# Batch 1's queries and keys made beside batch 0's softmax, in an attention and mixture-of-experts kernel

## The chip, the cores and the metric

The kernel runs on one core of a Trainium2 chip. The metric is device time in microseconds (us) of one execution. Engines are named as in the profile: PE (TensorE; PEld is its weight load), DVE (VectorE), ACT (ScalarE), POOL (GpSimd), SP (SyncE, which here only issues DMAs; its rows are SPq).

## What is computed

```python
def _L0_xattn_ref(teacher_logits, teacher_features, Wq, bq, Wk, bk):
    query = jnp.einsum('bnc,dc->bnd', teacher_features, Wq) + bq
    key = jnp.einsum('bnc,dc->bnd', teacher_features, Wk) + bk
    energy = jnp.einsum('bnd,bmd->bnm', query, key)
    attention = jax.nn.softmax(energy, axis=-1)
    return jnp.einsum('bln,bmn->blm', teacher_logits, attention)

x = x + _L0_xattn_ref(_layernorm(x), ctx_1024, Wq, bq, Wk, bk)
x = x + _L0_ffn_ref(_layernorm(x), ...)   # top 4 of 32 experts, SwiGLU, weighted sum
```

There are 4 batches of 1024 rows with 1024 features; the context has 512 features and queries and keys have 128. The expert part picks 4 of 32 experts for each row from logits that are taken in f32.

## The kernel before

Two functions run one after the other: `attention_and_routing` (the first 716 us) and `experts` (the rest, not touched). In the first, everything goes by tiles of 128 rows, eight tiles a batch, and each engine has a program of its own that is ordered by `schedule`; the engines meet only through semaphores.

`prepare` transposes the weights (into WT and gateT) and the context of batch 0 (`context`, four pairs of tiles, through the PSUM tensor psT into cxT), makes queries and keys (`queries_and_keys`: four quarters of 512 columns, two of queries and two of keys, each of four products, evacuated by DVE into qk at L813) and starts the first `energies`.

A `step(s, b1, b2, more)` then does two things that belong to different batches. The softmax half is for tile s of batch b1: `energies` into psE (L599), maximum (L822) and its negative on DVE, exponent on ACT (L522) into prob, layer norm of x on DVE (L792 to L797, the power of the variance on POOL), the scale of the probabilities (L827, L828), then both results cut into two f16 parts: the high parts on ACT (L529, L531), the low parts on DVE (L834 ah, L837 xnh or xg), and two DMA transposes issued by SP (L408, L413) into AT (printed W) and XT. The product half is for tile s of batch b2: 48 products (L651) into psM, the residual add on DVE (L896, xr, semaphore s_x2), layer norm 2 (LN2, into xs), then one step later its eight transposes on PE (L604, into psT), their evacuation on ACT (L540, x2T), eight logit products (L613) and the top-4 work on DVE.

Three kinds of steps follow each other. In the eight steps of batch 0 there is no product half; below they are called the lone steps. In `both`, from step 1 of the next round on, the LN2 transposes and logit products stand between the 48 products. The last ten steps have only a product half. At step 7 of a round PE makes the next batch's queries and keys and the first energies, in one piece. The context of the next batch is transposed in steps 2 to 5 (`CTX_STEPS`), also in the lone round.

The lines around which the change turns:

```python
quarter = [psM[:, 0:HALF], psM[:, HALF:], psE[:, 0:HALF], psE[:, HALF:]]
held = range(10, 10 + KH)          # LN2 transposes stand before these products of a step's first half
def next_batch():                  # step 7, PE
    alone(pe, s_exp, tile(b1, NT), s_past)
    alone(pe, s_x2, tile(b2, NT), s_past)
    queries_and_keys(following(b1))
```

Of the kernel before, what the change touches and what calls it, by code (L numbers as in the profile page):

```python
# [13 lines left out]
P = 128  # L14
# [119 lines left out]
def attention_and_routing(nc, g):  # L134
# [8 lines left out]
    with ExitStack() as ctx:  # L143
# [79 lines left out]
        quarter = [psM[:, 0:HALF], psM[:, HALF:], psE[:, 0:HALF], psE[:, HALF:]]  # L223
# [11 lines left out]
        s_wTev = sem("w_evacuated")  # L235
        s_x2out = [sem(f"x2_out{t}") for t in range(2)]
# [48 lines left out]
        CTX_STEPS = range(2, 2 + NT // 2)  # L285

# [20 lines left out]
        def lagged(bk, s, lag):  # L307

            if bk is None:
                return None  # L310
            if s >= lag:
                return (bk, s - lag) if s - lag < NT else None
            return None if first(bk) else ((bk[0], bk[1] - 1), NT + s - lag)

# [31 lines left out]
        def _(sp):  # L346
# [10 lines left out]
            sp.dma_start(wqk_in[:, 0, :], g["Wq"]).then_inc(s_small, 16)  # L357
            sp.dma_start(wqk_in[:, 1, :], g["Wk"]).then_inc(s_small, 16)
# [4 lines left out]
            load_ctx(0)  # L363
# [134 lines left out]
        def _(act):  # L498
            for n in range(2 * KC + KH):
                act.wait_ge(s_wT, n + 1)  # L500
                if n < 2 * KC:
                    act.activation(WT[:, n // KC, n % KC, :], psT[:, n % 2 * HALF:n % 2 * HALF + D], ACT.Copy).then_inc(s_wTev, 1)
                else:
                    act.activation(gateT[:, n - 2 * KC, :], psT[:, n % 2 * HALF:n % 2 * HALF + E], ACT.Copy).then_inc(s_wTev, 1)

            def context(bk, pair):
                act.wait_ge(s_cT, per(NT // 2, bk, pair + 1))
                act.activation(cxT[:, :, pair * 2 * P:(pair + 1) * 2 * P].rearrange("p c (t q) -> p t c q", t=2),
                               psT[:, :].rearrange("p (t c q) -> p t c q", t=2, c=KC), ACT.Copy).then_inc(s_cTev, 1)

            def prepare():
                for pair in range(NT // 2):
                    context((0, 0), pair)
                act.wait_ge(s_padout, 16 * 5)

            def step(s, b1, b2, more):
# [31 lines left out]
                if b1 is not None:  # L548
                    guarded(act, own, exponent)
                    if b2 is None and s - 1 in CTX_STEPS:  # L550
                        context(following(b1), s - 1 - CTX_STEPS[0])
# [30 lines left out]
        def _(pe):  # L582
            pe.wait_ge(s_const, 8)
            pe.wait_ge(s_small, 16 * 6)
            for n in range(2 * KC + KH):
                if n >= 2:
                    pe.wait_ge(s_wTev, n - 1)
                dst = psT[:, n % 2 * HALF:]
                if n < 2 * KC:
                    pe.transpose(dst[:, 0:D], wqk_in[:, n // KC, n % KC * P:(n % KC + 1) * P], ident[:]).then_inc(s_wT, 1)  # L590
                else:
                    k = n - 2 * KC
                    pe.transpose(dst[:, 0:E], gate_in[:, k * P:(k + 1) * P], ident[0:E, 0:E]).then_inc(s_wT, 1)
            pe.wait_ge(s_wTev, 2 * KC + KH)
# [22 lines left out]
            def context(bk, pair):  # L617

                if pair == 0:
                    alone(pe, s_ctx, per(16, bk, 16), s_past)  # L620
                for t in range(2):
                    for c in range(KC):
                        op = pe.transpose(psT[:, t * HALF + c * P:t * HALF + (c + 1) * P],
                                          cx[:, 2 * pair + t, c * P:(c + 1) * P], ident[:])
                op.then_inc(s_cT, 1)

            def queries_and_keys(bk):

                pe.wait_ge(s_cTev, per(NT // 2, bk, NT // 2))
                for n in range(4):  # L630
                    for c in range(KC):
                        op = pe.matmul(quarter[n], WT[:, n // 2, c, :], cxT[:, c, n % 2 * HALF:(n % 2 + 1) * HALF],
                                       start=c == 0, stop=c == KC - 1)
                    op.then_inc(s_qk, 1)
                pe.wait_ge(s_qkev, per(4, bk, 4))
                energies(0)

            def prepare():
                for pair in range(NT // 2):
                    if pair:  # L640
                        pe.wait_ge(s_cTev, pair)
                    context((0, 0), pair)
                queries_and_keys((0, 0))

# [66 lines left out]
            def step(s, b1, b2, more):  # L711
# [38 lines left out]
                if b1 is not None:  # L750
                    if s in CTX_STEPS:
                        if s - 1 in CTX_STEPS:
                            pe.wait_ge(s_cTev, per(NT // 2, following(b1), s - CTX_STEPS[0]))
                        guarded(pe, more, lambda: context(following(b1), s - CTX_STEPS[0]))
                if b2 is not None and s < NT:
                    product(product_of(s, b1), b2, s, 1, range(KH // 2, KH)).then_inc(s_xm, 1)
                if b1 is not None:
                    if b2 is not None:
                        guarded(pe, own, next_energies)
                    if s == NT - 1:  # L760
                        def next_batch():

                            alone(pe, s_exp, tile(b1, NT), s_past)
                            if b2 is not None:
                                alone(pe, s_x2, tile(b2, NT), s_past)
                            queries_and_keys(following(b1))
                        guarded(pe, more, next_batch)
# [14 lines left out]
        def _(dve):  # L782
# [24 lines left out]
            dve.wait_ge(s_small, 16 * 6)  # L807
            dve.wait_ge(s_wTev, 2 * KC + KH)

            def queries_and_keys(bk):  # L810
                for n in range(4):
                    dve.wait_ge(s_qk, per(4, bk, n + 1))
                    dve.tensor_scalar(qk[:, n // 2, n % 2 * HALF:(n % 2 + 1) * HALF], quarter[n],  # L813
                                      bqk[:, n // 2:n // 2 + 1], None, ALU.add).then_inc(s_qkev, 1)

            def step(s, b1, b2, more):
                own = more if s < 2 else None

                def maximum_and_norm():
# [3 lines left out]
                    dve.tensor_scalar(nmx[:, 0:1], mx[:, 0:1], -1.0, None, ALU.mult).then_inc(s_nmx, 1)  # L823
                    dve.wait_ge(s_x1[s % 2], per(8 * NT, b1, 16 * (s // 2 + 1)))
# [6 lines left out]
                def lo_parts():  # L831
# [42 lines left out]
                if b1 is not None:  # L874
# [435 lines left out]
```

## Time and profile before

| | us |
|---|---|
| median of 3 runs | 3167.7 (3167.55 to 3170.44) |
| time of the profiled execution | 3168.07 |
| its span in the profile | 3166.0 |
| PE busy | 3023.1 (95%) |
| DVE busy | 1710.9 (54%) |
| ACT busy | 1187.7 (38%) |
| POOL busy | 562.4 (18%) |

The busy shares are means over stages with different limits, so the table alone says little about the first 716 us: there, each stretch has to be read by itself. In a row of a timeline the first number is the start, the second how long the row lasts, then engine, line, operation, and in brackets how long the engine had been idle and whose result ended that.

### The profile page before, as it was taken

Reading aid. Unit: us, or ns where it says so; the run is one execution under the profiler, and the core shown is the slowest. Engines: PE = TensorE matmul, PEld = TensorE weight load, DVE = VectorE, ACT = ScalarE, POOL = GpSimd, SP = SyncE. Lnnn points to the kernel's source line nnn. Section 1 sums busy time; section 2 is a strip of 40 time slices with the busy share of each in tenths; the row PEclk is TensorE's granted clock in tenths of the full one; section 3 lists DMA queues with packets and bytes.
Section 4 is the critical chain, followed back from the end, with each engine's and each line's share of the span. In section 5 each row is a group of like instructions: output and inputs, shape, how many; then the busy total and the mean of one; then the engine's idle time right before and its main releaser. Section 6 shows DMA issues by size and latency. Waiting matters only on the chain.

```text
span 3166.0 us, 44613 instructions
## 1 busy us (share of the span) xinstructions
PE 3023.1 (95%) x14944; PEld 1547.1 (49%) x14945; DVE 1710.9 (54%) x2851; ACT 1187.7 (38%) x1235; POOL 562.4 (18%) x502
## 2 busy tenths in 40 slices
PE   6798988979999999999999999999999999999997
PEld 2354544544454454455445445445455544544543
DVE  3687878664454544555544545555454544554532
ACT  2342423223343434344443434444343433442422
POOL 1022323331111111111111111111111111111111
PEclk8899999989999999999999999999999999999999
DMA  6766656555554555656555656665556555565432
GB/s 191 176 176 184 176 145 182 159 167 161 158 153 113 163 151 154 196 159 179 171 141 153 195 146 190 183 186 152 155 161 191 153 155 157 153 180 132 116 64 60
DMA packets 343541, 501.36 MB, mean 158 GB/s; under 512 B 190881, under 2 KB 190881, under 8 KB 343234
## 3 DMA queue, kind: packets, MB, share of 16 engines
q10 hardware_dynamic: 94576, 225.46, 21.5%
q0 software_dynamic: 45856, 152.33, 21.3%
q1 hardware_dynamic: 203058, 122.94, 14.7%
q8 instruction: 25, 0.41, 0.1%
q14 instruction: 26, 0.21, 0.0%
HBM read 354.64 MB, written 112.46 MB: 148 GB/s over the span
## 4 chain that ended last, share of the span: by engine, by line
PE 75%; DMA 1%; issue 0%; ACT 0%; DVE 0%; SPq 0%; POOL 0%; ACTq 0%; POOLq 0%
PE psG L1226 23%; PE psU L1226 23%; PE psY L1248 23%; PE psX L1232 4%; PE psA L1239 2%; DMA acc<-y,idxs 0%; DMA idxs<-slots 0%; DMA stage<-in_L_ffn_w_gate 0%; ACT xT L1092 0%; DVE y L1171 0%; ACT y L1103 0%; POOL acc L1083 0%; SPq L1019 0%; ACTq L1016 0%; SPq L1020 0%
## 5 line engine op out<-in xcount | busy, mean ns | idle before, releaser
L1226 PE MATMUL psG<-W,xT 128*128 128x512 f16 x3456 | 770.8, 379 | 2.9 <-ACT xT L1092 2.8
L1248 PE MATMUL psY<-W,aT 128*128 128x512 f16 x3456 | 769.4, 379 | 1.5 <-ACT aT L1096 1.4
L1226 PE MATMUL psU<-W,xT 128*128 128x512 f16 x3456 | 769.4, 379 | 0.0
L1226 PEld LDWEIGHTS psG<-W,xT 128*128 128x128 f16 x3456 | 338.1, 98 | 412.3 <-issue 3.9
L1248 PEld LDWEIGHTS psY<-W,aT 128*128 128x128 f16 x3456 | 338.0, 98 | 377.3 <-ACT aT L1096 1.9
L1226 PEld LDWEIGHTS psU<-W,xT 128*128 128x128 f16 x3456 | 338.1, 98 | 375.7
L127 DVE SCALAR_TENSOR_TENSOR W<-stage,W 128x2048 f16<-128x2048 f32 x192 | 438.6, 2284 | 6.9 <-ACT W L122 6.7
L1171 DVE SCALAR_TENSOR_TENSOR y<-bias,idxs,y 128x1024 f32<-128x1024 f32 x143 | 183.7, 1285 | 462.3 <-ACT y L1103 462.3
L1059 POOL DMA_INDIRECT acc<-y,idxs x143 | 224.9, 1573 | 1006.4 <-DVE y L1171 966.9
L122 ACT ACTIVATE W<-stage 128x2048 f16<-128x2048 f32 x192 | 365.9, 1905 | 51.0 <-issue 38.2
L651 PE MATMUL psM<-W,XT 128*128 128x512 f16 x1392 | 355.9, 379 | 8.6 <-DVE xr L896 8.6
L1103 ACT ACTIVATE y<-psY,idxs 128x1024 f32<-128x1024 f32 x143 | 159.3, 1114 | 521.6 <-DMA idxs<-slots 518.2
L1054 POOL DMA_INDIRECT xg<-xn_tab,idxg x145 | 154.0, 1062 | 1051.7 <-PE psX L1232 649.0
L1092 ACT ACTIVATE xT<-psX 128x1024 f32<-128x1024 f32 x145 | 148.6, 1025 | 435.0 <-PE psX L1232 434.8
L1179 DVE SCALAR_TENSOR_TENSOR gt<-psG,bias 128x512 f32<-128x512 f32 x144 | 99.6, 692 | 364.6 <-PE psG L1226 340.4
L1190 DVE SCALAR_TENSOR_TENSOR up<-psU,bias 128x512 f32<-128x512 f32 x144 | 99.6, 692 | 301.0 <-PE psU L1226 301.0
L1139 ACT ACTIVATE sg<-gt 128x512 f32<-128x512 f32 x144 | 90.8, 631 | 444.1 <-DVE gt L1182 443.9
L651 PEld LDWEIGHTS psM<-W,XT 128*128 128x128 f16 x1392 | 149.4, 110 | 128.8 <-DVE xr L896 11.2
L485 POOL DMA_INDIRECT slots<-pack,dest x128 | 139.5, 1090 | 207.8 <-DVE tok L871 169.9
L1232 PE MATMUL psX<-ident,xg 128*128 128x128 f32 x1160 | 151.2, 274 | 15.6 <-PEq L143 15.6
L1232 PEld LDWEIGHTS psX<-ident,xg 128*128 128x128 f32 x1160 | 136.5, 142 | 44.2 <-DMA xg<-xn_tab,idxg 16.5
L522 ACT ACTIVATE stage<-psE,nmx 128x1024 f32<-128x1024 f32 x32 | 35.7, 1115 | 254.3 <-DVE nmx L823 254.3
(140 smaller groups left out, 2180.8 us busy)
## 6 DMA issues: line engine op xcount, KB each, us to landing
stage<-in_L_ffn_w_down ACTq DMA_DIRECT2D x62, 1024.0 KB, 6.3
stage<-in_L_ffn_w_up ACTq DMA_DIRECT2D x61, 1024.0 KB, 7.4
stage<-in_L_ffn_w_gate ACTq DMA_DIRECT2D x60, 1024.0 KB, 9.5
stage<-in_x SPq DMA_DIRECT2D x32, 512.0 KB, 5.3
xr<-in_x SPq DMA_DIRECT2D x32, 512.0 KB, 4.6
acc<-xr SPq DMA_DIRECT2D x32, 512.0 KB, 3.9
xn_tab<-x2h SPq DMA_DIRECT2D x32, 512.0 KB, 3.0
bias<-in_L_ffn_b_down ACTq DMA_DIRECT2D x32, 512.0 KB, 7.1
```

The source lines that it names most:

```text
L122: act.activation(W[:, par, HI, c * CHUNK:(c + 1) * CHUNK], stage[:, c % RING, :], ACT.Copy, scale=S_W).then_inc(s_whi, 1)
L127: dve.scalar_tensor_tensor(out=W[:, par, LO, c * CHUNK:(c + 1) * CHUNK], in0=stage[:, c % RING, :], scalar=S_W, in1=W[:, par, HI, c * CHUN ...
L485: pool.indirect_dma_start(out=slots[:, :], out_offset=bass.IndirectOffsetOnAxis(dest[:, n % 2, k:k + 1], 0), in_=pack[:, n % 2, k, :], in_ ...
L651: op = pe.matmul(out[:, h * HALF:(h + 1) * HALF], XT[:, a, k, t * P:(t + 1) * P], AT[:, par(bk), c, k, h * HALF:(h + 1) * HALF].rearrange( ...
L1054: pool.indirect_dma_start(out=xg[:], out_offset=None, in_=xn_tab[:, :], in_offset=bass.IndirectOffsetOnAxis(idxg[:, 0:1].bitcast(U32), 0)) ...
L1059: pool.indirect_dma_start(out=acc[:, :], out_offset=bass.IndirectOffsetOnAxis(idxs[:, 0:1].bitcast(U32), 0), in_=y[:], in_offset=None, com ...
L1092: act.activation(xT[:].rearrange("p k q a -> p (k q a)").bitcast(F32), psX[:], ACT.Copy).then_inc(s_xTev, 1)
L1103: act.activation(y[:], psY[:], ACT.Copy, scale=idxs[:, 2:3].bitcast(F32)).then_inc(s_y0, 1)
L1171: dve.scalar_tensor_tensor(out=y[:], in0=bias[:, par, 2 * I:], scalar=idxs[:, 1:2].bitcast(F32), in1=y[:], op0=ALU.mult, op1=ALU.add).then ...
L1226: op = pe.matmul(ps[:], xT[:, k, :, a], weights(par, c, offset + k * I, I), start=k == 0 and n == 0, stop=k == KH - 1 and n == 2)
L1232: op = pe.transpose(psX[:, n * P:(n + 1) * P], xg_w[:, n * P:(n + 1) * P], ident[:])
L1248: op = pe.matmul(psY[:, h * HALF:(h + 1) * HALF], aT[:, k, :, a], weights(par, c, 2 * KH * I + k * H + h * HALF, HALF), start=k == 0 and n ...
```

## The change

It has four parts, all in `attention_and_routing`.

1. **Start.** Wq and Wk get a semaphore of their own (s_wqk), and the context of batch 0 is loaded third on SP and not seventh. The eight weight transposes go into all of psT and leave in one evacuation. The four context pairs go into psM, psE, psT and psM, so only the fourth waits for an evacuation. The gate's transposes move behind the queries and keys.
2. **Lone round.** The context of batch 1 is transposed in steps 0 to 3, and one quarter of its queries and keys is made in each of steps 4 to 7, into the halves of psM, psQ and psR. DVE does the low parts of tile s-1 after the maximum of tile s (in step 7 also its own low parts), and the exponent waits for the low part of the probabilities, since it overwrites prob. At the end of step 7 only the four evacuations and the first energies are left.
3. **LN2 transposes** in `both` stand before products 16 to 23 and no longer 10 to 17, and the logit products before products 4 to 11 of the second half and no longer 2 to 9.
4. **Batches 2 and 3.** The queries' two quarters go into psE, and wait only for the last exponent; the keys' quarters go into psM and wait for the residual add (s_x2).

```diff
-        quarter = [psM[:, 0:HALF], psM[:, HALF:], psE[:, 0:HALF], psE[:, HALF:]]
+        psE_halves, psM_halves = [[ps[:, 0:HALF], ps[:, HALF:]] for ps in (psE, psM)]
+        early = psM_halves + [psQ[:, :], psR[:, :]]
+        first_pairs = [psM, psE, psT, psM]
...
+        CTX_ALONE = range(NT // 2)
+        QK_ALONE = range(NT // 2, NT)
+        QK_ORDER = (0, 2, 1, 3)
...
+        def quarter(bk, n):
+
+            if batch(bk) == 0:
+                return (psM_halves + psE_halves)[n]
+            return early[n] if batch(bk) == 1 else (psE_halves + psM_halves)[n]
...
-            sp.dma_start(wqk_in[:, 0, :], g["Wq"]).then_inc(s_small, 16)
-            sp.dma_start(wqk_in[:, 1, :], g["Wk"]).then_inc(s_small, 16)
+            sp.dma_start(wqk_in[:, 0, :], g["Wq"]).then_inc(s_wqk, 16)
+            sp.dma_start(wqk_in[:, 1, :], g["Wk"]).then_inc(s_wqk, 16)
+            load_ctx(0)
...
-            load_ctx(0)
...
                 def exponent():
                     act.wait_ge(s_nmx, tile(b1, s + 1))
+                    act.wait_ge(s_alo, tile(b1, s))
...
             def queries_and_keys(bk):
 
                 pe.wait_ge(s_cTev, per(NT // 2, bk, NT // 2))
                 for n in range(4):
...
+                    if n == 0 and not first(bk):
+                        pe.wait_ge(s_exp, NT * batch(bk))
+                    if n == 2 and not first(bk):
+                        pe.wait_ge(s_x2, NT * (batch(bk) - 1))
+                    one_quarter(bk, n)
...
-                held = range(10, 10 + KH)
+                held = range(16, 16 + KH)
...
-                    if m == 2:
+                    if m == 4:
...
-                    if 2 <= m < 2 + KH:
-                        logits_block(m - 2)
+                    if 4 <= m < 4 + KH:
+                        logits_block(m - 4)
...
+                if b1 is not None and b2 is None:
+                    if s == 0:
+                        pe.wait_ge(s_wTev, 2)
+                    if s in CTX_ALONE:
+                        if s > 0:
+                            pe.wait_ge(s_cTev, per(NT // 2, following(b1), s))
+                        context(following(b1), s)
+                    if s in QK_ALONE:
+                        n = QK_ORDER[s - QK_ALONE[0]]
+                        pe.wait_ge(s_cTev, per(NT // 2, following(b1), NT // 4 * (n % 2 + 1)))
+                        one_quarter(following(b1), n)
...
                     if s == NT - 1:
-                        def next_batch():
-
-                            alone(pe, s_exp, tile(b1, NT), s_past)
-                            if b2 is not None:
-                                alone(pe, s_x2, tile(b2, NT), s_past)
-                            queries_and_keys(following(b1))
-                        guarded(pe, more, next_batch)
+                        pe.wait_ge(s_exp, tile(b1, NT))
+                        first_energies(following(b1))
...
                     dve.tensor_scalar(nmx[:, 0:1], mx[:, 0:1], -1.0, None, ALU.mult).then_inc(s_nmx, 1)
+                    if b2 is None and s > 0:
+                        lo_parts(s - 1)
...
-                if b1 is not None:
+                if b1 is not None and (b2 is not None or s == NT - 1):
                     guarded(dve, own, lo_parts)
```

**Where instructions move.** First PE's program at the very start; stage holds the weights as loaded, W the context. Before:

```order
L590 MATMUL psT<-ident,stage 128x128 [waits small_in,consts]
L590 MATMUL psT<-ident,stage 128x128
L590 MATMUL psT<-ident,stage 128x128 [waits w_evacuated] x6
L593 MATMUL psT<-ident,stage 128x32 [waits w_evacuated] x8
L623 MATMUL psT<-ident,W 128x128 [waits ctx_in,w_evacuated,dve_consts]
L623 MATMUL psT<-ident,W 128x128 x7
L623 MATMUL psT<-ident,W 128x128 [waits ctxT_evacuated]
```

The same stretch of the changed kernel:

```order
L601 MATMUL psT<-ident,stage 128x128 [waits wqk_in,consts]
L601 MATMUL psT<-ident,stage 128x128 x7
L633 MATMUL psM<-ident,W 128x128 [waits ctx_in,w_evacuated,dve_consts]
L633 MATMUL psM<-ident,W 128x128 x7
L633 MATMUL psE<-ident,W 128x128 x8
L633 MATMUL psT<-ident,W 128x128 x8
L633 MATMUL psM<-ident,W 128x128 [waits ctxT_evacuated]
```

Twenty-four context transposes now stand in a row without a wait, and the gate's eight have gone behind the queries and keys.

Second, DVE's program in one lone step, from one maximum to the next. Before:

```order
L822 TENSOR_REDUCE mx<-psE 128x1 [waits energy_done]
L823 TENSOR_SCALAR nmx<-mx 128x1 [waits softmax_chain]
L792 BN_STATS st<-stage 128x6 [waits x1_in1]
L792 BN_STATS st<-stage 128x6
L794 BN_AGGR mv<-st 128x2 [waits ln1_chain]
L795 TENSOR_SCALAR ve<-mv 128x1 [waits ln1_chain]
L797 TENSOR_SCALAR stage<-stage,mv,rstd 128x1024 [waits rstd1_ready]
L827 RECIPROCAL sc<-psm 128x1 [waits exp_done]
L828 TENSOR_SCALAR sc<-sc 128x1 [waits softmax_chain]
L834 SCALAR_TENSOR_TENSOR ah<-stage,sc,ah 128x1024 [waits prob_scale_ready,prob_hi]
L837 SCALAR_TENSOR_TENSOR xg<-stage,xg 128x1024 [waits ln1_hi]
L822 TENSOR_REDUCE mx<-psE 128x1 [waits energy_done]
```

In the changed kernel:

```order
L845 TENSOR_REDUCE mx<-psE 128x1 [waits energy_done]
L846 TENSOR_SCALAR nmx<-mx 128x1 [waits softmax_chain]
L859 SCALAR_TENSOR_TENSOR ah<-stage,sc,ah 128x1024 [waits prob_scale_ready,prob_hi]
L862 SCALAR_TENSOR_TENSOR xnh<-stage,xnh 128x1024 [waits ln1_hi]
L815 BN_STATS st<-stage 128x6 [waits x1_in1]
L815 BN_STATS st<-stage 128x6
L817 BN_AGGR mv<-st 128x2 [waits ln1_chain]
L818 TENSOR_SCALAR ve<-mv 128x1 [waits ln1_chain]
L820 TENSOR_SCALAR stage<-stage,mv,rstd 128x1024 [waits rstd1_ready]
L852 RECIPROCAL sc<-psm 128x1 [waits exp_done]
L853 TENSOR_SCALAR sc<-sc 128x1 [waits softmax_chain]
L845 TENSOR_REDUCE mx<-psE 128x1 [waits energy_done]
```

The two low parts, which belong to the tile before, have come between the negative maximum and the statistics.

Third, PE's program from the last lone energies to the first products. Before, it is eight products into psM and eight into psE in one piece. In the changed kernel:

```order
L608 MATMUL psE<-stage 128x512 [waits exp_done]
L608 MATMUL psE<-stage 128x512
L639 MATMUL psM<-W,WT 128x512 [waits ctxT_evacuated]
L639 MATMUL psM<-W,WT 128x512 x3
L639 MATMUL psR<-W,WT 128x512 [waits ctxT_evacuated]
L639 MATMUL psR<-W,WT 128x512 x3
L608 MATMUL psE<-stage 128x512 [waits qk_evacuated,exp_done]
L608 MATMUL psE<-stage 128x512
L675 MATMUL psM<-W,XT 128x512 [waits ln1T_in0,probT_in1,probT_in0]
```

The last two quarters (steps 6 and 7) now stand ahead of the wait for the evacuations, and nothing but the energies is behind it. PE's products count twice in the trace: one f32 product of 512 columns shows as two rows' worth (x2).

## Rows read from the trace of the kernel before

**Rows 1.** The page, part 4: the chain that ended last, by line.

```profile
PE psG L1226 23%; PE psU L1226 23%; PE psY L1248 23%; PE psX L1232 4%; PE psA L1239 2%; DMA acc<-y,idxs 0%; DMA idxs<-slots 0%; DMA stage<-in_L_ffn_w_gate 0%; ACT xT L1092 0%; DVE y L1171 0%; ACT y L1103 0%; POOL acc L1083 0%; SPq L1019 0%; ACTq L1016 0%; SPq L1020 0%
```

**Rows 2.** Windows: length, busy us of each engine, PE's granted clock, DMA share, GB/s.

```profile
0.00:46.87 46.87, 31.64 (x84) 16.86 (x85) 7.35 (x12) 8.94 (x22) 5.75 (x20) 1.00 0.59 216
46.87:106.37 59.50, 30.55 (x60) 13.77 (x60) 44.12 (x77) 26.76 (x32) 3.86 (x7) 0.67 0.77 168
106.37:128.89 22.52, 18.88 (x37) 7.96 (x38) 9.39 (x16) 3.30 (x4) 0.55 (x1) 0.81 0.91 210
128.89:569.18 440.29, 394.63 (x2012) 225.44 (x2010) 348.57 (x1061) 144.82 (x196) 123.44 (x134) 1.00 0.64 170
```

**Rows 3.** DMA issues (KB, median us to landing) and PE's timeline, 0 to 45 us.

```profile
W<-in_ctx SPq DMA_DIRECT2D x2, 2048.0 KB, 9.9
stage<-in_L_xattn_Wk SPq DMA_DIRECT2D x1, 256.0 KB, 3.1
14.70 1.94 PE L623 MATMUL psT<-ident,W 128*128 128x128 f32 x8 [1.81 <-DMA W<-in_ctx]
...
27.00 10.13 PE L632 MATMUL psM<-W,WT 128*128 128x512 f32 x16 [1.11 <-ACT W L508]
...
44.85 1.98 PE L599 MATMUL psE<-stage 128*128 128x512 f32 x4 [0.84 <-DVE stage L813]
```

**Rows 4.** Timeline of one lone step (s = 1), from maximum to maximum.

```profile
55.33 1.22 DVE L822 TENSOR_REDUCE mx<-psE 128x1 f32<-128x1024 f32 x1
...
56.65 1.27 DVE L792 BATCH_NORM_STATS2 st<-stage 128x6 f32<-128x512 f32 x2
56.77 1.11 ACT L522 ACTIVATE stage<-psE,nmx 128x1024 f32<-128x1024 f32 x1 [2.86 <-DVE nmx L823]
...
58.03 3.78 PE L599 MATMUL psE<-stage 128*128 128x512 f32 x4 [5.07 <-ACT stage L522]
...
60.07 0.15 DVE L828 TENSOR_SCALAR sc<-sc 128x1 f32<-128x1 f32 x1
...
61.44 1.28 DVE L834 SCALAR_TENSOR_TENSOR ah<-stage,sc,ah 128x1024 f16<-128x1024 f32 x1 [1.22 <-ACT ah L529]
...
63.77 1.22 DVE L822 TENSOR_REDUCE mx<-psE 128x1 f32<-128x1024 f32 x1
```

**Rows 5.** Window over the same step, columns as in rows 2.

```profile
55.33:63.77 8.44, 3.78 (x4) 1.17 (x4) 6.30 (x12) 3.30 (x4) 0.55 (x1) 0.60 0.87 186
```

**Rows 6.** Timeline of step 7 of the lone round: queries and keys, and SP.

```profile
109.16 10.00 PE L632 MATMUL psM<-W,WT 128*128 128x512 f32 x16 [5.57 <-ACT stage L522]
...
113.87 7.51 SPq L408 DMA_TRANSPOSE W<-ah  x1
```

**Rows 7.** Timeline of PE where batches 2 and 3 begin.

```profile
261.57 8.80 PE L632 MATMUL psM<-W,WT 128*128 128x512 f32 x16 [3.21 <-DVE xr L896]
...
278.08 1.98 PE L599 MATMUL psE<-stage 128*128 128x512 f32 x4 [0.84 <-DVE stage L813]
...
416.93 7.10 PE L632 MATMUL psM<-W,WT 128*128 128x512 f32 x16 [3.18 <-DVE xr L896]
...
431.74 1.98 PE L599 MATMUL psE<-stage 128*128 128x512 f32 x4 [0.84 <-DVE stage L813]
```

**Rows 8.** PE's waits between 128 and 620 us, and one `both` step.

```profile
PE psT L604 <- DVE xs L797: 25.2, 21, 1.3
...
173.95 2.33 PE L651 MATMUL psM<-W,XT 128*128 128x512 f16 x10 [0.37 <-DVE xr L896]
...
177.62 0.30 PE L604 MATMUL psT<-ident,xs 128*128 128x128 f32 x1 [1.34 <-DVE xs L797]
...
181.14 1.00 ACT L540 ACTIVATE x2T<-psT 128x1024 f32<-128x1024 f32 x1
...
182.19 0.41 PE L613 MATMUL psR<-gateT,x2T 128*128 128x32 f32 x2
...
190.18 1.22 DVE L896 SCALAR_TENSOR_TENSOR xr<-psM,xr 128x1024 f32<-128x1024 f32 x1
```

More of the change, by code:

```diff
@@ L498, in _ @@
         def _(act):
[L499 to L504, printed above, removed]
+            act.wait_ge(s_wT, 1)
+            act.activation(WT[:, :, :, :].rearrange("p w c d -> p (w c d)"), psT[:], ACT.Copy).then_inc(s_wTev, 1)
             def context(bk, pair):
                 act.wait_ge(s_cT, per(NT // 2, bk, pair + 1))
+                ps = first_pairs[pair] if first(bk) else psT
                 act.activation(cxT[:, :, pair * 2 * P:(pair + 1) * 2 * P].rearrange("p c (t q) -> p t c q", t=2),
-                               psT[:, :].rearrange("p (t c q) -> p t c q", t=2, c=KC), ACT.Copy).then_inc(s_cTev, 1)
+                               ps[:, :].rearrange("p (t c q) -> p t c q", t=2, c=KC), ACT.Copy).then_inc(s_cTev, 1)
             def prepare():
@@ L549, in step @@
                     guarded(act, own, exponent)
-                    if b2 is None and s - 1 in CTX_STEPS:
-                        context(following(b1), s - 1 - CTX_STEPS[0])
+                    if b2 is None and s - 1 in CTX_ALONE:
+                        context(following(b1), s - 1)
                 if late:
@@ L583, in _ @@
             pe.wait_ge(s_const, 8)
[L584 to L594, printed above, removed]
+            pe.wait_ge(s_wqk, 16 * 2)
+            for n in range(2 * KC):
+                op = pe.transpose(psT[:, n * D:(n + 1) * D], wqk_in[:, n // KC, n % KC * P:(n % KC + 1) * P], ident[:])
+            op.then_inc(s_wT, 1)
+            pe.wait_ge(s_wTev, 1)
             pe.wait_ge(s_ready, 1)
@@ L620, in context, with one_quarter @@
                     alone(pe, s_ctx, per(16, bk, 16), s_past)
+                ps = first_pairs[pair] if first(bk) else psT
                 for t in range(2):
                     for c in range(KC):
-                        op = pe.transpose(psT[:, t * HALF + c * P:t * HALF + (c + 1) * P],
+                        op = pe.transpose(ps[:, t * HALF + c * P:t * HALF + (c + 1) * P],
                                           cx[:, 2 * pair + t, c * P:(c + 1) * P], ident[:])
                 op.then_inc(s_cT, 1)
+            def one_quarter(bk, n):
+                for c in range(KC):
+                    op = pe.matmul(quarter(bk, n), WT[:, n // 2, c, :], cxT[:, c, n % 2 * HALF:(n % 2 + 1) * HALF],
+                                   start=c == 0, stop=c == KC - 1)
+                op.then_inc(s_qk, 1)
             def queries_and_keys(bk):
@@ L630, in queries_and_keys, with first_energies @@
                 for n in range(4):
[L631 to L634, printed above, removed]
+                    if n == 0 and not first(bk):
[3 more added lines that the diff above has]
+                    one_quarter(bk, n)
+            def first_energies(bk):
                 pe.wait_ge(s_qkev, per(4, bk, 4))
@@ L639, in prepare @@
                 for pair in range(NT // 2):
-                    if pair:
-                        pe.wait_ge(s_cTev, pair)
+                    if pair == 3:
+                        pe.wait_ge(s_cTev, 1)
                     context((0, 0), pair)
                 queries_and_keys((0, 0))
+                pe.wait_ge(s_small, 16 * 4)
+                for k in range(KH):
+                    op = pe.transpose(psT[:, k * E:(k + 1) * E], gate_in[:, k * P:(k + 1) * P], ident[0:E, 0:E])
+                op.then_inc(s_wT, 1)
+                first_energies((0, 0))
             def product(out, bk, t, h, blocks, beside=None):
@@ L806, in _ @@
             dve.memset(psm[:], 0.0).then_inc(s_seen, 1)
-            dve.wait_ge(s_small, 16 * 6)
-            dve.wait_ge(s_wTev, 2 * KC + KH)
+            dve.wait_ge(s_small, 16 * 4)
+            dve.wait_ge(s_wTev, 1)
             def queries_and_keys(bk):
-                for n in range(4):
-                    dve.wait_ge(s_qk, per(4, bk, n + 1))
-                    dve.tensor_scalar(qk[:, n // 2, n % 2 * HALF:(n % 2 + 1) * HALF], quarter[n],
+                for done, n in enumerate(quarter_order(bk)):
+                    dve.wait_ge(s_qk, per(4, bk, done + 1))
+                    dve.tensor_scalar(qk[:, n // 2, n % 2 * HALF:(n % 2 + 1) * HALF], quarter(bk, n),
                                       bqk[:, n // 2:n // 2 + 1], None, ALU.add).then_inc(s_qkev, 1)
```

15 lines of the change are left out of this document (7 added, 8 removed).

## The prediction

> **What bounds the kernel now.** I read the chain that ended last first. It is PE nearly throughout, in lines of the experts [rows 1], which the change does not touch: their 2450 us move as a block. So only the first 716 us can change, and what is won there is won in full, since the experts begin when routing is done. The windows split that part [rows 2]. In the start (0 to 46.87) and in the lone round (46.87 to 106.37) PE is busy for 31.6 and 30.6 us only and no engine is full: these are chains of waits. Step 7 of the lone round takes 22.52 us, 18.88 of them PE's. The product rounds (128.89 to 569.18) look like PE's at 394.6 of 440.3 us, but the step itself says otherwise: DVE's residual add at 190.18 had no idle time before it, so DVE came straight from other work, while PE waited 0.37 us for it at 173.95 and 1.34 us for LN2 at 177.62 [rows 8]. DVE is the bound there, and PE's 25.2 us of waits for LN2 are mostly slack.
>
> **Start.** Before, PE waits for the context until 14.70, transposes four pairs with an evacuation behind each, starts queries and keys at 27.00 and the first energies at 44.85 [rows 3]. The context is now issued third, about 1.9 us earlier; a 2 MB load lands a median 9.9 us after issue [rows 3], and I take a start of the transposes at 12.2. The weights land 3.1 us after issue [rows 3], long before. Three of four pairs no longer wait: 4 x 1.94 = 7.8 us [rows 3], then one evacuation, for which I take the 1.1 us of idle ahead of 27.00 [rows 3]: queries and keys start near 20.8. Sixteen pieces took 10.13 us there at first, where PE had been interrupted before, and 7.10 us at 416.93 where it was warm [rows 3, 7]. The granted clock reads 1.00 over the whole start [rows 2], but 10.13 against 7.10 us for the same pieces means that part of them ran at 1.2 GHz. With 32 transposes in one run ahead of them I expect the 2.4 GHz pace from the first one: 431.74 - 416.93 = 14.8 us to the first energies [rows 7]. That gives 35.6, or **9.3 us** less. Bounds: context at 13.5 and the slow pace kept (17.85 us) give 4.5 us; context at 11.1 and fast transposes give 11.3 us. The gate's eight transposes hide behind the last evacuation (0.84 us idle [rows 3]).
>
> **Lone round.** DVE's chain from maximum (55.33) to the end of the scale (60.22) is 4.89 us; from the low part (61.44) to the next maximum (63.77) 2.33 us [rows 4]. What goes is the wait for ACT's high part between them, 1.22 us, because it now falls under the next maximum. DVE's cycle becomes 4.89 + 2.33 = 7.2 us against 8.44 [rows 5]. But the exponent now stands behind the low part: it starts at 1.33 (statistics at 56.65 less 55.33) + 1.28 = 2.65 us after the maximum, not at 1.44; the energies follow 1.26 us behind (56.77 to 58.03) and take 3.78 us [rows 4]: the next maximum can start at 7.7. So the loop through PE, at a granted clock of 0.60 [rows 5], is the longer one; at the 1.98 us of warm energies [rows 7] it would be 5.9 and DVE's 7.2 decides. DMA is third: a share of 0.87 of 8.44 us [rows 5] is 7.3 us of work in a step, mostly transposes. Steps 1 to 3, with 2 us of context transposes each, I put at 7.6. In step 4 a quarter follows the energies: eight pieces at 10.13/16 to 0.85 us are 5 to 6.8 us, so PE is busy on end, rises to 2.4 GHz (sixteen pieces in 10.00 us at 109.16, in 7.10 warm [rows 6, 7], say it does within them), and steps 5 and 6 go at DVE's or DMA's 7.3. Step 0 has no low parts before its statistics: exponent at once, 6.1 us. Sum for the seven steps: 6.1 + 4 x 7.6 + 2 x 7.3 = 51.1 against 59.50 [rows 2]: **8.4 us**. Bounds: all at 7.75 gives 6.9, all at DVE's 7.2 about 10.
>
> The Trainium skill, page "DMA: Bandwidth & Descriptors", section "Latency and other measured facts", gives 261 GB/s for a DMA transpose. By that figure the 1 MB of a step would be an estimated 4 us and DMA would be no bound; the step's rows show 186 GB/s at a share of 0.87, so the measurement decides, and DMA stays in the sum at 7.3.
>
> **Step 7 of the lone round.** After its maximum DVE does the low parts of tile 6, its own statistics and scale (7.1), waits for the high part, its own low parts (8.5 to 10.9), then four evacuations of ready quarters, 0.7 us each: energies at 13.7. PE has been idle for some 8 us then, so they cost 3.78, not 1.98: next maximum at 17.4 against 22.52 [rows 2], 5.1 us less. The first products then start at the low clock too, 1.2 us lost. The ctx load and the last probability transposes (issued 7.51 us long at 113.87 [rows 6]) land near 20 us, before the second half of the products asks for them near 23. Net **3.9 us**, bounds 2 and 5.
>
> **Batches 2 and 3.** PE is idle 3.21 and 3.18 us for the residual add, then needs 16.51 and 14.81 us to the energies [rows 7]; the first time the clock has dropped (8.80 us for sixteen pieces against 7.10). Now the queries start when the products end, at 258.4 and 413.8, and PE stays warm. The products themselves end 0.4 us earlier, as two more stand ahead of the logits. Energies at 272.9 and 428.2: 5.2 and 3.5 us, less 0.1 each for a later x2T: **8.5 us**, bounds 7 and 9.5.
>
> **LN2 transposes six products later.** From 173.95 sixteen products (0.21 us each, 10 in 2.33) reach 177.4, so the wait of 1.34 us nearly goes [rows 8]. But x2T is evacuated at 181.14 because ACT has the exponent and x2h before it, and logits start at 182.19 either way; the transposes, done near 180.2, leave 0.9 us. And DVE's loop does not pass through them. I give it 0.2 us in the one step where DVE still waited for PE, and nothing in the other 22.
>
> Sum: 9.3 + 8.4 + 3.9 + 8.5 + 0.2 = 30.3 us. The sum is made against the profiled execution's 3168.07, which is 0.4 above the median of the runs: **3137.8 us**. The terms' bounds add up to 20.4 and 36.0 us, 3132 to 3148.
>
> **Rivals.** (a) *DMA becomes the bound.* With the share at 1 the transposes of the lone round queue up, the low parts' buffers come free late, and step 7's land after the products want them, behind the 2 MB context. The share was 0.91 in that step [rows 2], which speaks for it; that each transpose has more than a step until it is needed speaks against it. Lone steps at 8.2 leave 2 us of 8.4 and the transition nothing: 30.3 - 10.3 = 20 us, 3148. (b) *PE stays at 1.2 GHz.* Quarters at 6.8 us and energies at 3.78 make steps 4 to 6 PE's, 10.6 us each, 3 x 3.1 = 9.3 us lost, 3 more in the start: 18 us, 3150. Against it: PE rose within sixteen pieces both times [rows 3, 6]. The Trainium skill, page "TensorE: Matmul & The Clock Gate", section "HAM oscillation — how this bites in real kernels", warns that idle gaps between bursts throw PE back to 1.2 GHz again and again, which speaks against handing out the quarters one by one; that is this rival, and the trace agrees that lone energies are slow (clock 0.60). (c) *Slower.* If the postponed LN2 transposes end more than 0.9 us later than I put them, x2T, logits and then every one of the 23 `both` steps grow. It decides from 0.9 + 30.3/23 = 2.2 us: at 3 us, 23 x 2.1 - 30.3 = 18 us slower, 3186. Nothing in the rows makes them that late. (d) *No change*: the experts would have to wait for something other than routing; the chain shows no such wait [rows 1]. 3168.
>
> **How the numbers follow.** Forecast 0.80, (a) 0.08, (b) 0.05, (c) 0.03, (d) 0.02, and 0.02 for a gain over 36 us. Of this kernel a measurement tells 0.2% (6 us) from no change. Forecast, (a) and (b) are all faster: 0.94; no change 0.03 and slower 0.03. The range goes from 3131 to 3149, to take in (a) and the low bounds.
>
> **What would show it.** First energies near 35.6; maxima of the lone round 7.2 to 7.8 apart, with DVE's idle before the low part gone and a new one before the maximum where PE is slow; the maximum of step 7 and of the next step 17.4 apart; no idle of PE after the last product of a batch; residual adds in `both` as far apart as before and PE's wait for LN2 replaced by one before the logits. I am wrong if PE keeps the low clock through queries and keys at the start, or if steps 5 and 6 stand above 8.

## The result, and the profile after

The changed kernel takes 3136.78 us, median of 4 runs (3135.79 to 3139.09), against 3168.56 for the one before (median of 4 runs). The ratio is 0.9902, 95% interval 0.9889 to 0.9914: it is faster, by some 31.8 us, with 3137.8 predicted. The profiled execution took 3135.79 us, its span is 3133.8.

The same windows as in [rows 2], cut at the corresponding maxima and residual adds (columns as there):

```profile
0.00:35.83 35.83, 23.57 (x84) 13.65 (x85) 7.36 (x11) 6.58 (x8) 5.76 (x20) 1.00 0.75 282
35.83:86.07 50.24, 34.43 (x80) 16.32 (x81) 41.82 (x75) 24.66 (x30) 3.86 (x7) 0.80 0.85 181
86.07:103.65 17.58, 9.47 (x19) 3.69 (x18) 11.43 (x19) 5.40 (x6) 0.55 (x1) 0.73 1.07 260
103.65:535.11 431.46, 393.04 (x2012) 224.54 (x2010) 348.24 (x1061) 144.70 (x196) 123.45 (x134) 1.00 0.68 176
```

The four stretches have lost 11.0, 9.3, 4.9 and 8.8 us, 34.1 together. The experts' first transposes start at 682.41, from where the window to the end of the span is 2451.39 us long; before it was 2449.78 us (from 716.22). So 1.6 us came back behind the change, and 0.3 us more between the last of these windows and the experts (147.30 us against 147.04). Most of the 1.6 us is in one place: the first 24 products of the experts took 7.98 us and not 6.69. That is a varying clock and not the change: in another profile of the changed kernel (e12_changed_again) the same products took 6.83 us.

**Start.** PE's timeline; the rows answer to [rows 3]. A "piece" is one row of PE's in the trace (the x16 at the end of a line are sixteen of them); "warm" below means the pace at 2.4 GHz and "cold" that at 1.2 GHz.

```profile
12.72 1.94 PE L633 MATMUL psM<-ident,W 128*128 128x128 f32 x8 [6.40 <-DMA W<-in_ctx]
14.46 1.56 PE L633 MATMUL psE<-ident,W 128*128 128x128 f32 x8
15.86 1.04 PE L633 MATMUL psT<-ident,W 128*128 128x128 f32 x8
16.73 1.04 PE L633 MATMUL psM<-ident,W 128*128 128x128 f32 x8
18.97 7.13 PE L639 MATMUL psM<-W,WT 128*128 128x512 f32 x16 [1.20 <-ACT W L520]
...
33.81 1.98 PE L608 MATMUL psE<-stage 128*128 128x512 f32 x4 [0.24 <-DVE stage L836]
```

Eight transposes take 1.94 us at first and 1.04 us from the third pair on: that is the step from 1.2 to 2.4 GHz, in the transposes and no longer in the products, whose first sixteen pieces take 7.13 us.

**Lone round.** One step's timeline, against [rows 4]:

```profile
56.51 1.23 DVE L845 TENSOR_REDUCE mx<-psE 128x1 f32<-128x1024 f32 x1 [0.38 <-PE psE L608]
57.85 1.28 DVE L859 SCALAR_TENSOR_TENSOR ah<-stage,sc,ah 128x1024 f16<-128x1024 f32 x1
59.23 1.11 ACT L537 ACTIVATE stage<-psE,nmx 128x1024 f32<-128x1024 f32 x1 [0.89 <-DVE ah L859]
60.19 1.28 DVE L815 BATCH_NORM_STATS2 st<-stage 128x6 f32<-128x512 f32 x2
60.49 3.37 PE L608 MATMUL psE<-stage 128*128 128x512 f32 x4 [3.08 <-ACT stage L537]
63.89 1.23 DVE L845 TENSOR_REDUCE mx<-psE 128x1 f32<-128x1024 f32 x1
```

The low part has no idle time ahead of it any more. In its place DVE waits 0.38 us for the energies, since the exponent now starts 2.72 us after the maximum (59.23 less 56.51), behind the low part. Here is how the maxima stand apart in the two lone rounds, and behind them the two steps in which batch 1 begins (from the starts of L822 and L845):

| | s=0 | 1 | 2 | 3 | 4 | 5 | 6 | 7 | next |
|---|---|---|---|---|---|---|---|---|---|
| before | 8.46 | 8.44 | 8.52 | 8.52 | 8.53 | 8.51 | 8.52 | 22.52 | 15.04 |
| changed | 5.80 | 7.24 | 7.64 | 7.38 | 7.80 | 7.18 | 7.20 | 17.58 | 15.42 |

**Step 7.** PE, SP and DVE:

```profile
88.14 3.60 PE L639 MATMUL psR<-W,WT 128*128 128x512 f32 x8
...
93.57 0.70 SPq L370 DMA_DIRECT2D W<-in_ctx  x1
94.39 0.57 SPq L367 DMA_DIRECT2D stage<-in_x  x1
95.97 9.08 SPq L423 DMA_TRANSPOSE W<-ah  x1
...
99.85 3.75 PE L608 MATMUL psE<-stage 128*128 128x512 f32 x4 [8.11 <-DVE stage L836]
...
103.65 1.22 DVE L845 TENSOR_REDUCE mx<-psE 128x1 f32<-128x1024 f32 x1 [3.94 <-PE psE L608]
```

The queries and keys are done 8.11 us before the energies need them, and the energies then run at 1.2 GHz.

**Batches 2 and 3.** PE's timeline, against [rows 7]:

```profile
232.53 7.03 PE L639 MATMUL psE<-W,WT 128*128 128x512 f32 x16
239.40 7.03 PE L639 MATMUL psM<-W,WT 128*128 128x512 f32 x16
247.27 1.98 PE L608 MATMUL psE<-stage 128*128 128x512 f32 x4 [0.84 <-DVE stage L836]
...
382.59 7.03 PE L639 MATMUL psE<-W,WT 128*128 128x512 f32 x16
```

No idle time, and full pace from the first piece. The transition, from the maximum of step 7 to the first maximum of the next batch, now takes 27.1 us both times; it took 32.68 and 30.96.

**`both` steps.** PE's waits between 104 and 595 us, and one step, against [rows 8]:

```profile
PE psR L622 <- ACT x2T L555: 18.9, 21, 1.0
PE psM L675 <- DVE xr L921: 11.0, 20, 1.0
...
139.28 0.41 PE L622 MATMUL psR<-gateT,x2T 128*128 128x32 f32 x2 [0.70 <-ACT x2T L555]
```

The 25.2 us of waits for LN2 have become 18.9 us of waits for x2T and more for the residual add; the maxima of these steps still stand 17.5 us apart.

### The profile page after: what moved, and what is told of

The parts are those of the page before. It is cut to its first block, busy times and chain, and to the rows that moved or that the text cites. A ratio compares the mean times of both kernels' runs of the same rounds, so it can differ in the third digit from the quotient of the medians.

```text
span 3133.8 us, 44628 instructions
## 1 busy us (share of the span) xinstructions
PE 3009.1 (96%) x14944; PEld 1541.6 (49%) x14945; DVE 1710.8 (55%) x2851; ACT 1184.7 (38%) x1221; POOL 562.5 (18%) x502
## 4 chain that ended last, share of the span: by engine, by line
PE 77%; DMA 1%; issue 0%; ACT 0%; POOL 0%; ACTq 0%; DVE 0%; SPq 0%; POOLq 0%
PE psG L1251 24%; PE psU L1251 24%; PE psY L1273 23%; PE psX L1257 4%; PE psA L1264 2%; DMA stage<-in_L_ffn_w_gate 0%; DMA idxs<-slots 0%; DMA acc<-y,idxs 0%; ACT xT L1117 0%; POOL acc L1108 0%; DVE y L1196 0%; ACTq L1041 0%; ACT y L1128 0%; SPq L1044 0%; SPq L1045 0%
## 5 line engine op out<-in xcount | busy, mean ns | idle before, releaser
L1225 DVE SCALAR_TENSOR_TENSOR ahl<-av,ahl 128x512 f16<-128x512 f32 x144 | 105.4, 732 | 43.1 <-ACT ahl L1170 43.1
```

## The experiments

Each is an edit of the changed kernel, unless it says otherwise. Medians of one and the same kernel differ by 1 to 1.5 us between sets of runs (the changed kernel gave 3136.78 and 3137.96, the one before 3168.56 to 3170.0), so where a few us or less are at stake I go by the distances between maxima in the profile, which repeat within 0.05 us wherever PE's clock is the same.

**e1_ln2_back.** The LN2 shift undone.

```diff
-                held = range(16, 16 + KH)
+                held = range(10, 10 + KH)
-                    if m == 4:
+                    if m == 2:
-                    if 4 <= m < 4 + KH:
-                        logits_block(m - 4)
+                    if 2 <= m < 2 + KH:
+                        logits_block(m - 2)
```

> The changed kernel with its third part undone: LN2 transposes again before products 10 to 17, logits before products 2 to 9. My theory: DVE bounds these steps, PE's 25 us of waits for LN2 were slack; the median moves from 3136.8 to between 3136.5 and 3138, PE waits for xs again (about 1.3 us, 20 times) and residual adds stay as far apart. Rival: the moved transposes are part of the gain; then the time rises by up to 25 us, to 3150 or more.

3138.55 us, half a us above the range I had given and, at that spread, not told apart from the changed kernel. Its waits (104 to 600 us) are those of the kernel before:

```profile
PE psT L613 <- DVE xs L820: 25.2, 21, 1.3
```

and the steps are as far apart as with the shift, 17.5 us. What the shift moves is small and of both signs: the transitions take 27.54 and 27.53 instead of 27.10 us (the two products ahead of the logits), the first `both` step takes 15.76 instead of 15.41, but the step behind each transition takes 17.53 instead of 17.83. The rival of 25 us falls.

**e2_low_back.** The low parts back in their own step.

```diff
-                    if b2 is None and s > 0:
-                        lo_parts(s - 1)
-                if b1 is not None and (b2 is not None or s == NT - 1):
+                if b1 is not None:
```

> The changed kernel with the low parts of a lone step back in their own step, behind ACT's high part. Theory: lone steps return from 7.2 to 7.8 to 8.45 us (+9.1 over seven steps), while step 7 loses the 2.3 us of tile 6's low parts: +6.8, near 3143.6. Rival: DMA, at a share near 1 in these steps, is what spaces them; then the steps stay at 7.2 to 7.8 and the time falls by 2 us or stays.

3144.26 us. The lone steps take 8.44 to 8.53 us again and step 7 takes 15.17 us. So the whole gain per lone step is DVE's order; at that spacing the quarters and transposes beside it cost nothing.

**e3_qk_end.** All four quarters in step 7.

```diff
-                    if s in QK_ALONE:
-                        n = QK_ORDER[s - QK_ALONE[0]]
-                        pe.wait_ge(s_cTev, per(NT // 2, following(b1), NT // 4 * (n % 2 + 1)))
-                        one_quarter(following(b1), n)
+                    if s == NT - 1:
+                        pe.wait_ge(s_cTev, per(NT // 2, following(b1), NT // 2))
+                        for n in QK_ORDER:
+                            one_quarter(following(b1), n)
```

> The changed kernel, but all four quarters of batch 1's queries and keys in one piece in step 7 (their banks are free, so they still start before the last exponent). Theory: queries and keys need 17 us from the end of the last energies, first 1.2 then 2.4 GHz; maximum of step 7 to the next maximum 19.9 instead of 17.6, energies of steps 4 to 6 slow again (+1.1 in all), the products after them warm (-0.4): +3.0, near 3139.8. Rival: handing out the quarters one by one is the source of the whole gain there; then the distance returns to 22.5 and the time rises by 5 to 6 us. Other rival: handing them out costs clock; then it gets faster.

3139.27 us, within the spread of the changed kernel. In the profile step 7 takes 17.82 us, hardly more than 17.58, because the first quarter starts at 89.34 already, before that step's maximum (89.58), and warms up in 4.83 us:

```profile
89.34 4.83 PE L639 MATMUL psM<-W,WT 128*128 128x512 f32 x8
...
94.00 3.60 PE L639 MATMUL psQ<-W,WT 128*128 128x512 f32 x8
97.44 3.60 PE L639 MATMUL psM<-W,WT 128*128 128x512 f32 x8
...
100.87 3.60 PE L639 MATMUL psR<-W,WT 128*128 128x512 f32 x8
...
105.40 1.96 PE L608 MATMUL psE<-stage 128*128 128x512 f32 x4 [0.94 <-DVE stage L836]
```

The energies are then warm (1.96 us) and the step behind takes 15.02; steps 4 to 6 take 7.84, 7.72 and 7.81. Together with the step behind, that is 1.0 us slower, not 3.0. So step 7's gain comes from banks that are free: the products no longer wait for the last exponent. Handing them out over four steps adds about 1 us.

**e4_bank_back.** Batches 2 and 3 wait for the residual add first.

```diff
-            return early[n] if batch(bk) == 1 else (psE_halves + psM_halves)[n]
+            return early[n] if batch(bk) == 1 else (psM_halves + psE_halves)[n]
...
-                        pe.wait_ge(s_exp, NT * batch(bk))
+                        pe.wait_ge(s_x2, NT * (batch(bk) - 1))
...
-                        pe.wait_ge(s_x2, NT * (batch(bk) - 1))
+                        pe.wait_ge(s_exp, NT * batch(bk))
```

> The changed kernel with batches 2 and 3 again as before: queries into psM behind the residual add, keys into psE. Theory: PE is idle for 3.6 us again, the first time cold for 1.7 us, and each of the two transitions gets back what it won, 5.6 and 3.9 us: +9.4, near 3146.2. Rival: DVE's LN2 and evacuations set the end of these transitions, and the bank is worth less than 4 us.

3149.4 us, 12.6 more where I expected 9.4. The transitions take 32.68 and 34.00 us: 5.6 and 6.9 us more. The mechanism is as expected, with a larger second price, because this time the clock was low there too (before, these sixteen pieces took 7.10 us [rows 7]):

```profile
237.65 8.80 PE L639 MATMUL psM<-W,WT 128*128 128x512 f32 x16 [3.64 <-DVE xr L921]
...
393.31 10.12 PE L639 MATMUL psM<-W,WT 128*128 128x512 f32 x16 [3.64 <-DVE xr L921]
```

**e5_load_back.** The first context load seventh again (`load_ctx(0)` behind the load of gb).

> The changed kernel with the context of batch 0 loaded seventh again, behind the small loads. Theory: context transposes start at 14.6 and not 12.7, everything behind them shifts by 1.9 us: near 3138.7. Rival: the landing is set by the DMA engines and not by the issue, no change.

3138.23 us. The transposes start at 14.08. In the ten profiles whose start is that of the changed kernel they start anywhere from 12.61 to 14.26, 13.5 on average. The early load is issued 1.88 us sooner (at 1.85 and not 3.73), but it took 10.5 to 12.2 us to land in those ten and 10.1 us here. Inconclusive: the landing alone varies by 1.7 us, nearly as much as the earlier issue could win. Neither my theory nor the rival is shown.

**e6_pairs_back.** Four pairs through one bank pair.

```diff
-        first_pairs = [psM, psE, psT, psM]
+        first_pairs = [psT, psT, psT, psT]
...
-                    if pair == 3:
-                        pe.wait_ge(s_cTev, 1)
+                    if pair:
+                        pe.wait_ge(s_cTev, pair)
```

> The changed kernel with all four first context pairs through psT again, each behind the evacuation of the one before. Theory: transposes take 12.3 us and not 6.2 to the start of queries and keys (+6.1), and PE, interrupted, starts these at 1.2 GHz: their first sixteen pieces take 10.1 and not 7.0 us (+3.1): +9.2, near 3146.0. Rival: the clock rises by itself after the start whatever the transposes do; then only +6.1, near 3142.9.

3146.64 us. PE's timeline:

```profile
12.87 1.94 PE L633 MATMUL psT<-ident,W 128*128 128x128 f32 x8 [6.48 <-DMA W<-in_ctx]
15.93 1.97 PE L633 MATMUL psT<-ident,W 128*128 128x128 f32 x8 [1.11 <-ACT W L520]
...
25.17 9.74 PE L639 MATMUL psM<-W,WT 128*128 128x512 f32 x16 [1.11 <-ACT W L520]
```

The transposes start like the changed kernel's, but queries and keys start at 25.17 and not 18.97, and run their first sixteen pieces in 9.74 us and not 7.13. Interrupted transposes keep PE at 1.2 GHz. The products pay 2.6 us for it, and so do the transposes themselves: from their start to that of queries and keys PE is busy for 7.84 us here and for 5.05 us in the changed kernel, so of the 6.1 us between the two 2.8 are clock and only 3.3 are waits. The total is as expected, its parts are not: 5.4 us of clock and 3.3 of waits.

**e7_warm.** Eight unused products in the gap of step 7. They are added work and change no result.

```diff
                         pe.wait_ge(s_exp, tile(b1, NT))
+                        for _ in range(8):
+                            pe.matmul(psE[:, 0:HALF], WT[:, 0, 0, :], cxT[:, 0, 0:HALF], start=True, stop=True)
                         first_energies(following(b1))
```

> The changed kernel with eight unused f32 products of 512 columns into psE between the last quarter and the first energies of batch 1 (they write a bank that the energies write again). Theory: PE's 8.1 us of idle time cost it the clock; with them the energies take 1.98 and not 3.75 us and the next products run at 2.4 GHz: -2.2, near 3134.6. Rival: the products end after the evacuations and delay the energies, or the clock changes nothing; then 3136.8 or more.

3135.52 us.

```profile
99.50 1.98 PE L608 MATMUL psE<-stage 128*128 128x512 f32 x4 [1.16 <-DVE stage L838]
101.33 5.34 PE L675 MATMUL psM<-W,XT 128*128 128x512 f16 x24
...
107.42 5.34 PE L675 MATMUL psM<-W,XT 128*128 128x512 f16 x24 [0.75 <-DMA W<-ah]
```

The energies are warm and step 7 takes 15.72 us, 1.9 less. But the next step takes 15.93 and not 15.42: the second half of the products waits 0.75 us for the last probability transposes. A wait that was hidden has come out, and 1.3 us are left where I expected 2.2.

**e8_dma_more.** One more 512 KB load in each lone step, into x2h and xs2, which are unused there. (Lines that are not shown make ACT and DVE wait for these loads before the buffers are used again; the last load landed at 113.0, before the products that this run is about were done, so these waits are not what it measures.)

```diff
+                    if b2 is None:
+                        dst = (x2h[:, 0, :, :], x2h[:, 1, :, :])[s % 3] if s % 3 < 2 else xs2[:, :]
...
+                        sp.dma_start(dst, x_rows[0, s]).then_inc(s_extra[s % 3], 16)
```

> The changed kernel with one more load of 512 KB in each lone step, into buffers that are unused there. It adds some 1.4 us of work of all DMA engines to the 7.3 us of a step. Theory: transposes are not needed until two steps later, so the first lone steps keep 7.2 to 7.8 us, the backlog grows by 1.4 us a step, and only step 7 and the products behind it feel it: +3 to +8. Rival: DMA already bounds the lone steps; then each grows by 1.4 us, +11. Other rival: DMA is far from the bound, less than +1.

3146.43 us, 9.7 more, which is above my +3 to +8 and near the rival's +11. The steps tell the two apart: the lone ones behind step 0 take 7.18 to 7.84 us and step 7 17.58, as without the loads, but the step behind it 23.09 instead of 15.42:

```profile
101.67 10.99 SPq L424 DMA_TRANSPOSE W<-ah  x1
104.47 6.64 PE L686 MATMUL psM<-W,XT 128*128 128x512 f16 x24
...
114.91 8.20 PE L686 MATMUL psM<-W,XT 128*128 128x512 f16 x24 [3.80 <-DMA W<-ah]
```

The backlog is paid in one place, where the products first ask for tile 7's probabilities. It shows in SP's issues too: the last transpose of probabilities begins to be issued 14.5 us after the maximum of step 7 and not 9.9. The 7.7 us are 3.8 of wait and 3.9 of clock, for the first 24 products (6.64 us) and above all the second (8.20), against 5.34 warm. The clock is what I had left out.

**e9_ctx_late.** e7_warm, and the 2 MB context load behind step 7's transposes.

```diff
-                    if s == NT - 2:
+                    if s == NT - 1:
                         guarded(sp, None if first(b1) else b1[0] < B - 3, next_ctx)
```

> e7_warm with the 2 MB load of the next-but-one context issued behind the transposes of step 7 and not ahead of them. In e7_warm PE waited 0.75 us for the last probability transposes, which stood 11.7 us in the queue. Theory: that wait goes and they land within 6 us of issue; from the first maximum of batch 1 to the next 15.0 instead of 15.9: -0.9 against e7_warm, near 3134.5. Rival: the transposes are slow by themselves or the load then delays the next ones; no change.

3134.54 us, ratio 0.9891 (0.9875 to 0.9908).

```profile
96.87 2.98 SPq L423 DMA_TRANSPOSE W<-ah  x1
...
101.54 1.29 SPq L370 DMA_DIRECT2D W<-in_ctx  x1
102.49 10.52 PE L675 MATMUL psM<-W,XT 128*128 128x512 f16 x48
```

The transpose of tile 7's probabilities landed 4.9 us after its issue, in the changed kernel 11.2. The forty-eight products run without a break and the step takes 15.03 us, 0.9 less than in e7_warm, as expected.

**e10_lone_warm.** e9_ctx_late with one unused product in each of steps 0 to 3.

```diff
                         context(following(b1), s)
+                        pe.matmul(psR[:, :], WT[:, 0, 0, :], WT[:, 1, :, :].rearrange("p c d -> p (c d)"), start=True, stop=True)
```

> e9_ctx_late with one unused f32 product of 512 columns behind the context transposes of each of steps 0 to 3, into psR. Theory: PE is busy in some 80% of a step instead of 62% and keeps 2.4 GHz more often; energies take 1.98 and not 3.2 to 3.8 us, the maxima stand 7.2 apart, up to 1.5 us less than e9_ctx_late. Rival: the gap ahead of the energies remains, the clock falls as before, and the added product only stands in their way: 0 to +2.

3135.3 us. Steps 1 to 4 take 7.58, 7.18, 7.83 and 7.18 us, 29.8 together, in e9_ctx_late 7.41, 7.82, 7.18 and 7.20, 29.6. Nothing is won: PE still idles 2.3 to 3.5 us ahead of the energies, which took 3.56, 1.98 and 3.78 us in turn.

**e11_start_warm.** e9_ctx_late with three unused products of the same form while PE waits for the first context.

> e9_ctx_late with three unused f32 products into psR while PE waits for the first context (6.4 us idle). Theory: the context transposes start at 2.4 GHz and ACT's evacuations (four times 1.1 us) bound them: the first maximum comes at 35 to 36 in every profile and not anywhere from 35.8 to 38.8 as in the kernels so far: -1 to -2 against e9_ctx_late. Rival: the spread comes from when the context lands; no change.

3134.65 us. All four pairs take 1.04 to 1.07 us and the first maximum comes at 34.7, against 38.13 in e9_ctx_late. But step 0 takes 6.58 instead of 4.84 us and steps 3 and 4 are slow, so that at the maximum of step 7 only 1.3 us are left (85.7 against 87.0), and the median shows none of it. The spread of the start has two sources, then: when the context lands, and when PE rises to 2.4 GHz in the transposes (from their start to that of queries and keys the ten profiles take 6.25 to 7.70 us, this one 4.93).

**e12_changed_again.** The changed kernel, beside the last three.

> The changed kernel itself, beside e9 to e11 on the same chip. Its median should be 3136 to 3138. Its first maximum was at 35.83 in its profile, the earliest of seven kernels that start alike; I expect it nearer 37.3 this time, with the lone steps and transitions as before within 0.6 us.

3137.96 us. The first maximum comes at 38.39, then the steps take 4.84, 7.62, 7.81, 7.18, 7.84, 7.17, 7.20, 17.40 and 15.03 us. Step 0 is 0.96 us shorter than in the first profile, more than the 0.6 I allowed; the others lie within it. Beside it e9_ctx_late is 3.4 us faster (3133.61 to 3135.64 against 3137.79 to 3139.28). It is the best version found, though e10_lone_warm and e11_start_warm are not told apart from it.

## Why the prediction was right

| term | predicted | profile of the change |
|---|---|---|
| start | 9.3 | 11.0 (46.87 - 35.83) |
| lone round | 8.4 | 9.3 (59.50 - 50.24) |
| step 7, and the clock behind it | 3.9 | 4.6 (22.52 - 17.58 less 15.42 - 15.04) |
| batches 2 and 3 | 8.5 | 8.8 (5.58 + 3.85 less 2 x 0.30) |
| LN2 shift | 0.2 | 0.35 (15.76 - 15.41) |

Every term has the predicted sign and lies within its bounds but the last, which had none. The total is closer than its parts, and that is luck: the terms came out 3.7 us larger than predicted (34.05 against 30.3), 1.9 us came back behind them, in a stretch that I had taken to move as a block, and the median of the changed kernel lies 1.0 us above its profiled execution.

*Start.* That the transposes in one run warm PE up before the products is shown by e6_pairs_back, and by all ten profiles with the same start code: the first sixteen pieces took 7.13 us in each. The profile of the change was a lucky one. Over the ten the first maximum came at 35.83 to 38.78, 37.5 on average, which is 9.4 us of gain. That this average meets the 9.3 is luck as well, since two sizes were off and cancel. The transposes start at 13.5 on average and not at 12.2: 14.70 less 1.9 is 12.8 already, and the load, put at a median of 9.9, took 10.5 to 12.2 us. In return they and the last evacuation take 7.2 us and not 8.6, because PE warms up within them. (The prediction's own figures, 12.2, 7.8 and 1.1, add up to 21.1 and not to the 20.8 it gives.) The earlier load, of which I expected 1.9 us, is not shown to be worth so much (e5_load_back).

*Lone round.* Right in its mechanism: e2_low_back gives back exactly the 8.44 to 8.53 us. Of the three limits I saw, DVE's 7.2 and the 7.7 of PE's loop are visible, as steps of 7.18 to 7.20 where the energies are warm and up to 7.84 where they are not. Step 0 took 5.80 us and not 6.1, and 4.83 or 4.84 in profiles where its energies were warm. The third limit, DMA at 7.3, does not show in a step; e8_dma_more tells why: transposes are not needed for two more steps, so a full queue defers its price to step 7.

*Step 7.* 17.4 predicted, 17.58 measured, and the slow energies (3.75 us) came from 8.11 us of idle time, as e7_warm shows. Two sizes were off. The clock's price behind it is 0.4 and not 1.2 us, and 0 in e12_changed_again, where forty-eight products took 10.52 us in spite of 3.58 us for the energies. And I counted on 3 us of slack for the last transposes, landing near 20 and wanted near 23 us after the maximum. They landed at 107.2, 21.1 us after it, the second half of the products started at some 109.0, and 1.9 us earlier products were enough in e7_warm to lay 0.75 us of wait bare. Rival (a) was thus nearer than its 0.08 says: not in the lone steps, but in its second half, the landing of step 7's transposes behind the 2 MB context.

*Batches 2 and 3.* e4_bank_back confirms the term and prices the clock: behind the same 3.64 us of idle time the sixteen pieces took 1.7 us more than warm once and 3.0 us more once. Had the second one been cold in the kernel before, as it was in e4_bank_back, the term would have been 3 us larger.

*LN2 shift.* e1_ln2_back shows that 25.2 us of waits were slack but for tenths. The shift also has a price that I had at 0.1 and that was 0.3: in the step behind a transition x2T waits for the transposes, and the logits for x2T. That step was PE's to set, so its residual add came 13.1 and not 12.8 us after the maximum.

Rival (b), PE at 1.2 GHz throughout, did not come: PE warmed up within the first quarter (4.65 us for its eight pieces, then 3.60). Single energies behind idle gaps were cold in part (up to 3.78 us against 1.98), and that did not decide. Against rival (c) speaks that no `both` step grew apart from those 0.3 us.

## What to carry to other kernels

Read a step's own chain before adding up an engine's waits: 25 us of PE's waits here were worth tenths, while 1.2 us of DVE's idle time in a step without products was worth 1.1 us a step on average (0.7 to 1.3 in steps 1 to 6). When a bank or a buffer is what holds work back, freeing it gave nearly all of the gain (e3_qk_end, e4_bank_back), and spreading the work out further gave little. And look at which transfer stands ahead of the one that is due next: with all DMA engines full (a share of 1.07 in step 7), one 2 MB load was hidden until the stage before it got shorter.

## What the runs showed of the hardware that I had not expected

The same 2.8 us of idle time ahead of step 0's energies left PE warm in some profiles and cold in others. Where the first maximum came early (34.7 and 35.83), step 0 took 6.58 and 5.80 us; where it came late (37.6 to 38.8), step 0 took 4.83 or 4.84 us, its energies 1.98 us. So a first maximum 3.4 us earlier gained 1.3 us one stage on and nothing in the median (e11_start_warm). But being early is not the cause: in e6_pairs_back, where it came latest of all (44.64), step 0 took 6.47 us. What decides is not shown. Likewise, behind one and the same gap of 3.64 us sixteen pieces took 8.80 us once and 10.12 us once within one execution (e4_bank_back), and behind 3.18 us of idle time 7.10 us, the warm pace, at 416.93 [rows 7]. The granted clock reads 1.00 in the start of the profiles before and after, also where eight transposes take 1.94 us and later 1.04: there the durations tell the clock, not the column.
